# First layer of a fused graph network: ranking of edges cut into pieces, and the loop over pairs of graphs written out

## The reference, cut to what matters

```python
diff = e[:, :, :, None] - offsets                      # 64 offsets
g = jnp.exp(coeff * diff * diff)
h = ssp(jnp.einsum('bijg,fg->bijf', g, W1) + b1)       # ssp = softplus - ln 2
Wf = jnp.einsum('bijf,gf->bijg', h, W2) + b2
rf = jnp.einsum('bjd,fd->bjf', r, Wa)
Wf = Wf * A[:, :, :, None]
y = jnp.einsum('bjf,bijf->bif', rf, Wf * A[:, :, :, None])
y = ssp(jnp.einsum('bif,df->bid', y, Wd1) + bd1)
y = jnp.einsum('bid,ed->bie', y, Wd2) + bd2
x = _layernorm(x + y, axis=-1)
```

## Time and profile before

| what | before |
|---|---|
| median of 3 runs | 1319.08 us |
| profiled execution, its span | 1328.99 us, 1327.2 us |
| TensorE matmul busy | 1120.4 us, 84% of the span |
| VectorE busy | 918.7 us, 69% |
| ScalarE busy | 929.1 us, 70% |
| GpSimd busy | 723.0 us, 54% |
| instructions in the trace | 28,584 |
| data queue q1 | 127.19 MB, 46.0% of 16 engines over the span |
| instruction queues q8 and q14 | 33 packets of 0.54 MB, 55 packets of 0.45 MB |

### The profile page before, as it was taken

How to read it: one execution, slowest core, us unless ns; L and a number is a source line. 1 busy time by engine, 2 the same in 40 slices (tenths; PEclk the granted TensorE clock), 3 DMA queues, 4 the chain that set the end, 5 groups by cost and what they waited for, 6 DMA issues and landing times. The chain is left out here.

```text
span 1327.2 us, 28584 instructions
## 1 busy us (share of the span) xinstructions
PE 1120.4 (84%) x6028; PEld 770.1 (58%) x6028; DVE 918.7 (69%) x3889; ACT 929.1 (70%) x2685; POOL 723.0 (54%) x1258
## 2 busy tenths in 40 slices
PE   2588888888888888888874789999789999999974
PEld 1254554544554554444543577777568888887873
DVE  3588988989999988888853798998413333333357
ACT  2488888878888888888761688888535555555566
POOL 6276777766777777676664899998300000000036
PEclk9999999999999999999985899999789999999978
DMA  1788999878789799889920000000000000000013
GB/s 48 151 186 170 174 197 165 179 183 179 172 195 175 176 185 166 178 169 189 174 80 27 17 17 25 17 25 17 1 5 17 13 17 17 13 17 17 12 33 96
DMA packets 130489, 129.31 MB, mean 97 GB/s; under 512 B 61123, under 2 KB 111711, under 8 KB 130401
## 3 DMA queue, kind: packets, MB, share of 16 engines
q1 hardware_dynamic: 128676, 127.19, 46.0%
q10 hardware_dynamic: 1725, 1.13, 0.3%
HBM read 123.05 MB, written 5.21 MB: 97 GB/s over the span
## 5 line engine op out<-in xcount | busy, mean ns | idle before, releaser
L803 PE MATMUL wf<-hid,w2t 128*128 128x384 f32 x512 | 201.0, 516 | 61.2 <-DVE msg L979 61.2
L1810 POOL MEMSET r_minus_half<- 128x4 f32 x1 | 0.1, 102 | 307.7 <-POOLq L1652 307.7
L803 PEld LDWEIGHTS wf<-hid,w2t 128*128 128x128 f32 x512 | 87.7, 191 | 136.1 <-issue 102.3
L585 POOL TENSOR_TENSOR sum<-msg 128x384 f32<-128x384 f32 (+1 forms) x128 | 150.4, 1175 | 29.0 <-DVE msg L979 28.4
L979 DVE SCALAR_TENSOR_TENSOR msg<-wf,b2c,rv 128x768 f32<-128x768 f32 x128 | 129.8, 1014 | 10.0 <-PE wf L803 10.0
L696 ACT ACTIVATE expd<-zb,safe_b,reached 128x768 f32<-128x768 f32 x128 | 125.0, 977 | 2.6 <-PE zb L789 2.4
L1758 DVE SCALAR_TENSOR_TENSOR r_new<-r_gates 128x64 f32<-128x64 f32 x128 | 28.8, 225 | 141.4 <-ACT r_gates L1732 141.4
L952 DVE TENSOR_TENSOR rv<-rg,sq_bc 128x768 f32<-128x768 f32 x128 | 121.4, 948 | 2.7 <-PE rg L832 2.7
L701 ACT ACTIVATE hid<-expd 128x768 f32<-128x768 f32 x128 | 108.0, 844 | 17.7
L788 PE MATMUL zb<-gauss,w1t 64*128 64x384 f32 x256 | 117.8, 541 | 0.0
L789 PE MATMUL zb<-gauss,w1t 64*128 64x384 f32 x256 | 117.8, 541 | 0.0
(11 more groups left out here) (302 smaller groups left out, 3335.8 us busy)
## 6 DMA issues: line engine op xcount, KB each, us to landing
sq_bc<-edge_sq SPq DMA_DIRECT2D x64, 768.0 KB, 7.1
val_bc<-edge_val SPq DMA_DIRECT2D x128, 192.0 KB, 5.7
idx_bc<-edge_idx SPq DMA_DIRECT2D x64, 384.0 KB, 6.7
adj_w<-in_adj_rows SPq DMA_DIRECT2D x64, 64.0 KB, 6.4
xt_w<-in_x_cols SPq DMA_DIRECT2D x64, 64.0 KB, 6.1
xin<-in_x_rows SPq DMA_DIRECT2D x32, 128.0 KB, 6.5
m_adj_g<-in_adj_rows SPq DMA_DIRECT2D x16, 256.0 KB, 2.8
adjt<-in_adj_t SPq DMA_DIRECT2D x32, 128.0 KB, 2.1
```

The costliest lines, as they stand in the source:

```text
L585: pool.tensor_tensor(sum1[:, 0:wide, :], m[:, 0:wide, :], m[:, wide:2 * wide, :], ALU.add)\
L803: last = pe.matmul(wf[:, half, 0:HALF], w2t[:, :], hid[:, q, half * HALF:(half + 1) * HALF], start=True, stop=True)
```

## The change

Two things change, both in `layer0`.

The loop over pairs is written out on all engines: `body` is called for pairs -2 to 32 with constants in all addresses and wait values. No instruction of the work itself is added or removed.

`rank_edges` and `place_overflow` are cut into six pieces, with products of the current graph between them. In the order of VectorE's program, for the first unit: `pick`, first MAX8, `rv`, second piece (replace, index, MAX8), `t_h`, third piece (the same again), `msg`, `count_overflow` (count and last index). For the second unit: `pick`, the cast of the indices, `rv`, the copy of `p_start`, the residual sum, `cover_slots`, `msg`, `finish_edges`. On TensorE the small product `p_start` moves from before `wf` to behind it.

```diff
             else:
-                pairs(eng, (-2, -1, 0), (1, B // 2 - 3), (B // 2 - 3, B // 2 - 2, B // 2 - 1, B // 2), body)
+                for pair in range(-2, B // 2 + 1):
+                    body(pair)
...
-                    if not dense and k_in == 1 and g.has(4):
-
-                        w(pe, "cnt", g.at(4) + 1)
-                        if g.has(1):
-                            w(pe, "rfhi_ready", g.at(1) + 1)
-                        pe.matmul(p_start, before[:, :], over_cnt[:, bass.ds(g.at(4), 1)], start=True, stop=True)\
-                            .then_inc(s["start_ready"], 1)
                     if u.has(0):
 
                         w(pe, "hid_ready", u.at() + u0 + 1)
...
                         last.then_inc(s["wf_ready"], 1)
+                    if not dense and k_in == 1 and g.has(4):
+
+                        w(pe, "cnt", g.at(4) + 1)
+                        if g.has(1):
+                            w(pe, "rfhi_ready", g.at(1) + 1)
+                        pe.matmul(p_start, before[:, :], over_cnt[:, bass.ds(g.at(4), 1)], start=True, stop=True)\
+                            .then_inc(s["start_ready"], 1)
...
-            def rank_edges(g):
+            def first_ranks(g):
...
                 alone(dve)
+                dve.max(found[:, q, 0:8], adj_w[:, q, :]).then_inc(s["top1"], 1)
+
+            def second_ranks(g):
+
+                q, n = g.mod(2, 4), g.at(4) + 1
                 adj, ranked = adj_w[:, q, :], found[:, q, :]
-                dve.max(ranked[:, 0:8], adj).then_inc(s["top1"], 1)
                 w(dve, "top1", n)
...
                 dve.max(ranked[:, 8:16], adj_r1[:, :]).then_inc(s["top2"], 1)
+
+            def third_ranks(g):
+
+                n, ranked = g.at(4) + 1, found[:, g.mod(2, 4), :]
                 w(dve, "top2", n)
...
                 dve.max(ranked[:, 16:24], adj_r2[:, :]).then_inc(s["top3"], 1)
+
+            def count_overflow(g):
+
+                n, ranked = g.at(4) + 1, found[:, g.mod(2, 4), :]
                 w(dve, "top3", n)
...
                 dve.max_index(found_idx[:, 16:24], ranked[:, 16:24], adj_r2[:, :]).then_inc(s["idx3"], 1)
+
+            def convert_indices(g):
+
+                n = g.at(4) + 1
                 w(dve, "idx3", n)
                 alone(dve)
-                dve.tensor_copy(ranked[:, RANKS:2 * RANKS], found_idx[:, :]).then_inc(s["idxf"], 1)
+                dve.tensor_copy(found[:, g.mod(2, 4), RANKS:2 * RANKS], found_idx[:, :]).then_inc(s["idxf"], 1)
...
                 dve.tensor_copy(start, p_start).then_inc(s["start_copied"], 1)
+
+            def cover_slots(g):
+
+                n = g.at(4) + 1
+                start = found[:, g.mod(2, 4), 2 * RANKS:2 * RANKS + 1]
                 w(dve, "start_copied", n)
...
+                    if not dense and k_in == 0 and g.has(4):
+                        first_ranks(g)
+                    if not dense and k_in == 1 and g.has(4):
+                        convert_indices(g)
                     if u.has(0):
...
+                    if not dense and k_in == 0 and g.has(4):
+                        second_ranks(g)
                     if k_in == 0 and g.has(-2):
...
                     if not dense and k_in == 0 and g.has(4):
-                        rank_edges(g)
+                        third_ranks(g)
+                    if not dense and k_in == 1 and g.has(4):
+                        place_overflow(g)
                     if k_in == 1 and g.has(-2):
...
                     if not dense and k_in == 1 and g.has(4):
-                        place_overflow(g)
+                        cover_slots(g)
...
+                    if not dense and k_in == 0 and g.has(4):
+                        count_overflow(g)
```

## The result

The changed kernel takes 1312.21 us (median of 20 runs, 1304.83 to 1317.74), the kernel before 1319.82 us in the same comparison (20 runs, 1311.78 to 1326.83). The ratio is 0.9941, with a 95% interval of 0.9923 to 0.9959: faster by 0.6%, 7.6 us. The forecast was 17.4 us.

A forecast was written before the change was run, and what follows sets the result against it. SyncE's loop through memory was taken as the bound: 10.02 - 0.56 + 0.25 = 9.71 us a graph, 56 graphs by 0.31 us are 17.4 us, 1319.08 - 17.4 = 1301.7, say 1302 us; range 1268 to 1322 us.

The forecast's parts named there:

- The loop through memory sets the period: On SyncE, stores, their landing and the next values' load form a loop that sets the 10.02 us per graph.
- VectorE alone could just explain the period: VectorE's 9.26 us for one graph, with slower picks in many others, comes to about 10.0 us.
- the 0.56 us saved on SyncE: Register work gone from SyncE's loop: 0.41 us before the first store plus 0.15 before the values, per graph.
- the issue of the values to the first store: On SyncE, this step falls from 1.78 us in the loop to 1.37 written out, 0.41 saved.
- The engine is off the deciding loop, so this buys nothing by itself: Ranking in pieces cuts VectorE's period from 9.26 to about 8.25 us, without gain by itself.
- The 0.25 us for longer landings: Instruction fetches and tighter transfers lengthen the stores' landings by 0.25 us a graph, bounds 0 and 1.0.
- VectorE's four waits: VectorE's four waits for its own last result in the ranking go, 1.0 us a graph in sum.
- such a loss from its new place: On VectorE, pick behind count_overflow meets GpSimd's sum and costs 0.5 us a graph, bounds 0 and 1.4.
- TensorE's detour: With p_start behind wf, p_over starts 1.38 us after p_start; TensorE's floor becomes 9.1 us, between 8.94 and 9.59.
- The transfers wait for one another, not for SyncE: Rival: stores land only when earlier transfers drain, period stays near 10.0 us, 1317 us; chance 0.15.
- Landings don't grow: Rival: the stores' landings stay as long as before, period 9.46 us, 1288 us; chance 0.20.
- The slower rival: Code fetches lengthen the stores' landing; 1.0 us more gives 1344 us, deciding from 0.56 us of growth; chance 0.12.

The follow-up runs named there:

- e6: The changed kernel with separate semaphores for each of the three stores, so the load of the values waits for edge_val alone: 1299.73 us, 0.9824 of the kernel before.
- e13: The kernel before with only SyncE's program written out, ranking in the old order: 1322.24 us, 0.9993 of the kernel before.
- e1: The kernel before with only the loop over pairs written out on all engines, ranking in one piece: 1319.79 us, 0.9973 of the kernel before.
- e2: The changed kernel with the loop over pairs put back; ranking in pieces and p_start behind wf stay: 1320.42 us, 0.9975 of the kernel before.
- e3: The changed kernel with only SyncE written out, the other four engines running the loop: 1311.56 us, 0.9916 of the kernel before.
- e5: The changed kernel with SyncE loading the adjacency early, right behind the squares: 1311.94 us, 0.9939 of the kernel before.
- e15: The same kernel as e3, timed again on another occasion: 1307.87 us, 0.9881 of the kernel before.
- e7: The changed kernel with both the early adjacency of e5 and the separate semaphores of e6: 1298.35 us, 0.9829 of the kernel before.
- e8: As e7, but only SyncE is written out and the other four engines run the loop: 1299.71 us, 0.9815 of the kernel before.

## Why the prediction failed in size and held in direction

*The bound.* "The loop through memory sets the period": right, but it was half of the truth. `e6` shows that the landing decides in the changed kernel. `e13` and `e1` show that VectorE in its old order holds 9.90 us by itself. I had seen that "VectorE alone could just explain the period", and then used 9.26 for its own period.

*The step that failed: the 0.56 us saved on SyncE, taken in full from a period of 10.02.* In the profiles the period fell by 0.20 us, not by 0.31. The mis-sized term is the issue of the values to the first store: forecast 1.37 us, a saving of 0.41; measured on average 1.80 before and 1.52 after, a saving of 0.28. It is 1.35 in the median graph. But in 5 of 58 graphs the two issues take over 1.6 us, like the 1.79 above, where the loop had one such, and SyncE waited 3.4 us for `ei`. The other terms: store to values 7.14 - 0.15 + 0.25 = 7.24, measured 7.17; first to last store 1.10, measured 1.13. Sum 9.71, measured 9.82. By 56 graphs, 0.20 us are 11 us of the 17.4.

*From the profile to the median.* The rest of the shortfall, 11 to 7.6 us, is in the base. I took a gain worked out on an execution that was 9.9 us long and subtracted it from the median. `e13` took as long as the kernel before (0.9993), and its profile, of an execution inside its timed range (1319.28 us), has a period of 9.90. So at its median the kernel before had some 9.9 us too, an estimate, and there was less to gain from the start. Not all of the surplus was in the period: behind the last `edge_sq` store the profile of before took 671.1 us and that of `e13` 666.2. That the two profiles differ by 14.6 us, near the forecast, is in part luck.

*A step wrong beside it: "The engine is off the deciding loop, so this buys nothing by itself".* 9.26 us was VectorE's best graph. Writing SyncE out alone brought 0.07% (`e13`) and writing everything out 0.27% (`e1`), where the sum counted all of the gain on it, because VectorE's old order takes 9.9 on average. Both changes together brought 0.84% in the comparison of `e1` and `e2`, and 1.2% in that of `e13`. This alone does not explain the shortfall of the whole change: after it, VectorE had 34.1 us to spare, waiting for the adjacency. What the 0.25% of the pieces alone (`e2`) is made of isn't shown; SyncE's wait for `ei` was 3.3 us there and 3.0 before.

*The landings.* The 0.25 us for longer landings was right in size (6.78 to 7.01 for `edge_sq`), but the reason was not: SyncE's step from store to values is 7.18 us in `e3` too, which fetches hardly any code. That they lengthen as the transfers follow more closely is argued, not shown. The code fetched came to 0.73 MB more in the whole execution, forecast about 1.2.

*VectorE's four waits* are gone, as forecast, but its own period fell less. The graphs in which it waits for no one else take from 9.03 us after and from 9.26 before; the forecast was 8.75. The cast of the indices, which no longer waits, takes 0.41 us instead of 0.20. And `pick` takes longer, on average 0.671 instead of 0.536 us, 0.27 us for the two of a graph. The forecast took such a loss from its new place. The runs don't bear that out: with the pieces and VectorE still in its loop it is 0.510 (`e2`) and 0.506 (`e3`). It lengthens where the engines other than SyncE are written out, whose worth I had put at 0: from 0.506 to 0.671 with the pieces, from 0.626 (`e13`) to 0.712 (`e1`) in the old order. Why isn't shown. That the adjacency would be late for VectorE (34.1 us) I had not foreseen; `e5` shows it harmless.

*TensorE's detour* was right to 0.02 us: `p_over` starts 409.89 - 408.49 = 1.40 us after `p_start`, forecast 1.38. The floor made from it, 9.1 with a lower bound of 8.94, was too high: single graphs of `e2`, `e3` and `e15` take 8.65 us, in `e15` with TensorE idle for 0.66 us of it. The shortest graphs of the changed kernel, at 9.03 us, come near 9.1 by chance: VectorE works through them with gaps of 0.25 us at most in all, more nearly without a break than TensorE, which idles for 0.53. Neither floor decided, since the period stayed above it.

*Rivals.* "The transfers wait for one another, not for SyncE" had 1317 us. It has part of the truth: writing out SyncE alone gave nothing (`e13`), though by VectorE, not by the drain. "Landings don't grow": they grew. The slower rival: growth was 0.23 us, with or without fetches; it would have needed 0.56.

**A version that beats both** is `e7` or `e8`: 0.9829 and 0.9815 of the kernel before, in one comparison with `e5`, the changed kernel's like, at 0.9939. `e6`, with the semaphores alone, is as fast within the intervals (0.9824).

## What to carry to other kernels

Find the loops that pass through memory: a store, its landing, a load of other data that waits behind it in the same program. Their sum is the period even when every queue and engine looks merely busy, and the list of what the issuing engine waits for shows them. When two such chains are within 2% of each other, work out both with their bad graphs in, not with the best one; the gain of relieving one alone is what lies between them. And subtract a gain from the execution in which it was worked out; if that lies outside the timed runs, the gain may too. The same holds behind the result: the profile of `e6` was of its slowest execution and that of `e15` of its fastest, and neither may be set against a median.

## What the runs showed of the hardware

A 6 KB store took about 7 to 8 us from issue to landing beside this traffic, from SyncE's, GpSimd's or ScalarE's queue alike (8.0, 7.3 and 8.2 us for `edge_val`), and only 0.3 us less with 384 KB fewer ahead of it. The same 192 stores were 52,224 packets from SyncE or ScalarE and 6144 from GpSimd, with little difference in landing. Three stores on one semaphore are shown with 4.9, 5.7 and 6.8 us; on semaphores of their own the first of them took 8.0. Issues from SyncE that take 0.6 us each with register addresses (two in 1.45) take about as long with constants (two in 1.23); what goes is the register work around them, 1.77 to 1.35 us in the median from the values to the first store. `pick`, the same instruction throughout, took 0.50 to 0.63 us on average in the kernels in which VectorE ran its loop, and 0.66 to 0.71 where all engines were written out and SyncE issued the stores.
